# Up projection of a conditioned, quantised gated MLP: plain float32 products in place of three float32r products of high and low parts

## The reference

```python
scale = cond @ norm_w.T + 1.0                       # [32, 256]
ms = jnp.mean(x * x, axis=-1, keepdims=True)
h = x * (scale[:, None, :] * jax.lax.rsqrt(ms + EPS))
u = h @ up_w.T                                      # up_w [2048, 256]
val, gate = jnp.split(u, 2, axis=-1)
h = val * gelu(gate)                                # exact gelu, [.., 1024]
y = act_quant(h) @ weight_quant(down_w).T           # int8 rows, ternary weights
return y + x
```

## Time and profile before

| | |
|---|---|
| median of 2 runs | 430.2 us (430.07 to 430.33) |
| traced execution | 430.28 us, span 428.5 us |
| TensorE matmuls (PE) | 422.5 us busy, 99% of the span, 2081 records |
| TensorE weight loads (PEld) | 334.2 us, 78% |
| VectorE (DVE) | 283.4 us, 66% |
| ScalarE (ACT) | 189.6 us, 44% |
| GpSimd (POOL) | 192.1 us, 45% |

### The profile page before, as it was taken

How to read it: one execution, slowest core, us unless ns; L and a number is a source line. 1 busy time by engine, 2 the same in 40 slices (tenths; PEclk the granted TensorE clock), 3 DMA queues, 4 the chain that set the end, 5 groups by cost and what they waited for, 6 DMA issues and landing times.

```text
span 428.5 us, 7739 instructions
## 1 busy us (share of the span) xinstructions
PE 422.5 (99%) x2081; PEld 334.2 (78%) x2081; DVE 283.4 (66%) x539; ACT 189.6 (44%) x334; POOL 192.1 (45%) x323
## 2 busy tenths in 40 slices
PE   7999999999999999999999999999999999999997
PEld 5777777877877877777777777778778778777886
DVE  4887566576576575575675675665765765755776
ACT  5743444444444444444434444434444444444441
POOL 1565345345354354354454453453453543543520
PEclk9999999999999999999999999999999999999999
DMA  8424434334434334334244343244343344342324
GB/s 288 137 76 122 125 73 122 80 92 122 106 90 122 72 99 122 90 106 110 72 112 122 75 120 84 88 122 116 80 122 76 96 122 96 100 118 70 82 50 124
DMA packets 82024, 45.01 MB, mean 105 GB/s; under 512 B 68256, under 2 KB 68704, under 8 KB 81888
## 3 DMA queue, kind: packets, MB, share of 16 engines
q1 hardware_dynamic: 81584, 44.33, 40.0%
q10 hardware_dynamic: 432, 0.59, 0.4%
HBM read 20.00 MB, written 8.39 MB: 66 GB/s over the span
## 4 chain that ended last, share of the span: by engine, by line
PE 96%; DVE 1%; POOL 1%; DMA 1%; issue 0%; ACT 0%; DVEq 0%; POOLq 0%
PE p_gate L674 41%; PE p_val L674 41%; PE p_y L696 12%; PE p_gate L646 1%; PE p_val L646 1%; DMA cond_norm_sb<-cond_norm 1%; DVE y_sb L495 0%; PE p_gate L653 0%; POOL a_hi L306 0%; PE p_val L653 0%; POOL scaled L303 0%; PE p_y L621 0%; PE p_y L615 0%; DVE q_rounded L519 0%; DVE h L540 0%
## 5 line engine op out<-in xcount | busy, mean ns | idle before, releaser
L540 DVE SCALAR_TENSOR_TENSOR h<-p_val,rstd,gelu 128x512 f32<-128x512 f32 x128 | 95.4, 746 | 127.0 <-PE p_val L674 126.1
L384 ACT ACTIVATE gelu<-p_gate,rstd 128x512 f32<-128x512 f32 x128 | 88.1, 688 | 154.4 <-PE p_gate L674 144.0
L299 POOL TENSOR_TENSOR mean_sq_eps<-mean_sq,rms_eps 128x1 f32<-128x1 f32 x64 | 12.3, 192 | 213.1 <-PE p_val L674 198.8
L356 ACT ACTIVATE q<-q_rounded 128x1024 bf16<-128x1024 f32 x63 | 66.7, 1058 | 70.8 <-DVE q_rounded L578 70.8
L674 PE MATMUL p_gate<-up_hi,a_lo 128*128 128x512 f32 x248 | 83.0, 415 | 0.6 <-POOL a_lo L310 0.6
L564 DVE TENSOR_REDUCE h_max<-h 128x1 f32<-128x1024 f32 x63 | 76.9, 1220 | 2.2
L674 PE MATMUL p_val<-up_hi,a_hi 128*128 128x512 f32 x248 | 78.2, 396 | 0.0
L674 PE MATMUL p_gate<-up_hi,a_hi 128*128 128x512 f32 x248 | 78.1, 396 | 0.0
L674 PE MATMUL p_val<-up_hi,a_lo 128*128 128x512 f32 x248 | 78.1, 396 | 0.0
L674 PE MATMUL p_val<-up_lo,a_hi 128*128 128x512 f32 x248 | 78.1, 396 | 0.0
L674 PE MATMUL p_gate<-up_lo,a_hi 128*128 128x512 f32 x248 | 78.1, 395 | 0.0
(11 more groups left out here) (74 smaller groups left out, 249.3 us busy)
## 6 DMA issues: line engine op xcount, KB each, us to landing
xt_in<-x_t SPq DMA_DIRECT2D x32, 256.0 KB, 2.8
x_all<-x SPq DMA_DIRECT2D x32, 256.0 KB, 2.8
out<-y_sb SPq DMA_DIRECT2D x31, 256.0 KB, 2.2
up_raw<-up_w_t SPq DMA_DIRECT2D x6, 256.0 KB, 5.3
down_raw<-down_w_t SPq DMA_DIRECT2D x1, 1024.0 KB, 7.9
q_t<-q SPq DMA_TRANSPOSE x63, 3.1
up_raw<-up_w_t ACTq DMA_DIRECT2D x2, 256.0 KB, 3.3
out<-y_sb SPq DMA_DIRECT2D x1, 128.0 KB, 2.0
```

Source lines behind the costliest of these rows:

```text
L299: pool.tensor_tensor(mean_sq_eps[:, j:j + 1], mean_sq[:, j:j + 1], rms_eps[:, :], ALU.add).then_inc(pool_step, 1)
L356: act.activation(q[j % 2][:, :], q_rounded[j % 2][:, :], ACT.Copy, bias=-ROUND).then_inc(q_ready, 1)
L384: act.activation(gelu[c][:, :], p_gate[c][:, :], ACT.Gelu, scale=rstd[:, j:j + 1]).then_inc(gelu_done, 1)
L540: nc.vector.scalar_tensor_tensor(h[s][:, c * W:(c + 1) * W], p_val[c][:, :], rstd[:, j:j + 1], gelu[c][:, :], op0=ALU.mult, op1=ALU.mult). ...
```

## The change

The up products take the scaled x and the landed weights as they are, in plain float32: one product over two slices for a bank, 2 matmul calls in place of 6, 8 for a tile in place of 24. `a_hi`, `a_lo`, `up_hi`, `up_lo` and their semaphores are gone, and with them GpSimd's second multiplication and its subtraction, ScalarE's eight copies and VectorE's eight subtractions at the start, and `up_first`. Tiles 0 and 1 get their `scaled` from VectorE. The down products and everything behind the banks stay.

```diff
@@ GpSimd, tile
                 def product():
                     pool.tensor_tensor(scaled[s][:, :, :], xt_in[i][:, :, half, :], scale,
-                                       ALU.mult).then_inc(pool_step, 1)
-
-                    pool.tensor_tensor(a_hi[s][:, :, :], xt_in[i][:, :, half, :], scale,
-                                       ALU.mult).then_inc(pool_step, 1)
-
-                def low_part():
-                    pool.tensor_tensor(a_lo[s][:, :, :], scaled[s][:, :, :], a_hi[s][:, :, :].bitcast(fp32),
-                                       ALU.subtract).then_inc(a_ready, 1)
+                                       ALU.mult).then_inc(a_ready, 1)
...
@@ ScalarE, start
-            for c in range(NP * 2):
-                for k in range(KD):
-                    act.wait_ge(up_in[c * KD + k], 16)
-                    act.activation(up_hi[:, c, k, :], up_raw[:, c, k, :], ACT.Copy).then_inc(up_hi_ready, 1)
-                if c == 2:
-                    square(0, 0, True)
...
+            square(0, 0, True)
@@ VectorE, start
+            for j in range(2):
                 for k in range(KD):
...
+                    last = nc.vector.tensor_scalar(scaled[j][:, k, :], xt_in[0][:, k, j, :], scale_t[:, k, 0:1], None,
+                                                   ALU.mult)
                 last.then_inc(first_a_ready, 1)
...
-            for c in range(NP * 2 * KD):
...
-                nc.vector.tensor_tensor(up_lo[cols], up_raw[cols], up_hi[cols].bitcast(fp32),
-                                        ALU.subtract).then_inc(up_lo_ready, 1)
@@ TensorE, up
+                    if not (first and j == 0):
+
+                        pe.wait_ge(read, NP * (t - 1) + c + 1)
+                    for k in range(KD):
+                        if first and j == 0:
+
+                            pe.wait_ge(up_in[col * KD + k], 16)
+                        last = nc.tensor.matmul(bank[:, :], scaled[j % 2][:, k, :], up_raw[:, col, k, :],
+                                                start=(k == 0), stop=(k == KD - 1))
                     last.then_inc(done, 1)
```

More of the change, by code:

```diff
@@ L63, in build @@
         up_raw = sb("up_raw", [P, NP * 2, KD, W], fp32)
-        up_hi = sb("up_hi", [P, NP * 2, KD, W], fp32r)
-        up_lo = sb("up_lo", [P, NP * 2, KD, W], fp32r)
         down_raw = sb("down_raw", [P, KF, D], fp32)
@@ L82, in build @@
         scaled = [sb(f"scaled{i}", [P, KD, P], fp32) for i in range(2)]
-        a_hi = [sb(f"a_hi{i}", [P, KD, P], fp32r) for i in range(2)]
-        a_lo = [sb(f"a_lo{i}", [P, KD, P], fp32r) for i in range(2)]
         squares = [sb(f"squares{i}", [P, D], fp32) for i in range(2)]
@@ L137, in build @@
         scale_ready = sem("scale_ready")
-        up_hi_ready = sem("up_hi_ready")
-        up_lo_ready = sem("up_lo_ready")
         abs_ready = sem("abs_ready")
@@ L146, in build @@
         a_ready = sem("a_ready")
-        a_hi_ready = sem("a_hi_ready")
-        second_a_hi_ready = sem("second_a_hi_ready")
         squares_done = sem("squares_done")
@@ L279, in _ @@
             pool.wait_ge(scale_ready, 1)
-            BEFORE, PER_TILE = 3 + 2, 3
+            BEFORE, PER_TILE = 3 + 2, 1
             def tile(u, j, first):
@@ L319, in tile @@
                     product()
-                    pool.wait_ge(pool_step, step + 3)
-                    low_part()
+                    pool.wait_ge(pool_step, step + 1)
                 pool.tensor_tensor(rstd[:, j:j + 1], mean_sq_eps[:, j:j + 1], minus_half[:, :],
@@ L432, in _ @@
             dve.wait_ge(scale_ready, 1)
[L433 to L437, removed]
+            for j in range(2):
                 for k in range(KD):
-                    last = nc.vector.scalar_tensor_tensor(a_lo[j][:, k, :], xt_in[0][:, k, j, :], scale_t[:, k, 0:1],
-                                                          a_hi[j][:, k, :].bitcast(fp32),
-                                                          op0=ALU.mult, op1=ALU.subtract)
+                    last = nc.vector.tensor_scalar(scaled[j][:, k, :], xt_in[0][:, k, j, :], scale_t[:, k, 0:1], None,
+                                                   ALU.mult)
                 last.then_inc(first_a_ready, 1)
-            dve.wait_ge(a_hi_ready, KD)
-            low_part(0)
-            for c in range(NP * 2 * KD):
-                dve.wait_ge(up_hi_ready, c + 1)
-                cols = (slice(None), c // KD, c % KD, slice(None))
-                nc.vector.tensor_tensor(up_lo[cols], up_raw[cols], up_hi[cols].bitcast(fp32),
-                                        ALU.subtract).then_inc(up_lo_ready, 1)
-            dve.wait_ge(second_a_hi_ready, 1)
-            low_part(1)
             def ternary(stage):
@@ L624, in _ @@
             keep_busy(4)
[L626 to L655, removed]
             def up(u, j, c, first):
[L658 to L662, removed]
                 t = UNIT * u + j
-                if c == 0:
+                by_others = first and j < 2
+                if c == 0 and by_others:
+                    pe.wait_ge(first_a_ready, j + 1)
+                elif c == 0:
                     pe.wait_ge(a_ready, t - 1)
```

## The result

The changed kernel took 509.25 us, median of 2 runs (509.03 to 509.48), against 430.2 before: 1.184 times the time (95% interval 1.182 to 1.185). The forecast was 511 us, 1.19 times. The traced execution took 509.03 us, its span is 507.2 us.

A forecast was written before the change was run, and what follows sets the result against it. TensorE's stream was taken to bound the kernel, busy for 99% of the span. 430.28 us, plus 78.6 for tiles 2 to 63 and 2.0 at the start, gave 510.9: forecast 511 us, 1.19 times, range 506 to 552.

The forecast's parts named there:

- TensorE's stream is the time: Whole kernel: time is TensorE's stream plus a start and a tail; TensorE busy for 99% of the span.
- Sixteen records a tile: TensorE's up products: a plain float32 call becomes two matmul records, so 16 a tile against 24.
- Two streams per record: TensorE's up products: each record streams its 512 columns twice, 429 ns a record, 6.87 us a tile, 1.27 more.
- The float32r surcharge would not come back: TensorE's up products: plain float32 records pay 3 ns over their column slots, not float32r's 20 ns.
- Rival 1: TensorE's up products: surcharge stays, 467 ns a record (549 us, chance 0.24) or 447 ns (529 us, chance 0.17).
- The low level as a rival: TensorE in the loop: falls to its low level, 853 ns a record, 943 us; chance 0.04 with other dear cases.
- rival 3: TensorE stays at its low level, 853 ns a record, 943 us; chance 0.04 together with other dear cases.
- Start: Tiles 0 and 1: first up product at about 5.95 us, TensorE rises at 11.0, tile 2 begins at 22.4: +2.0 us.
- Down group: TensorE's down products in each tile: 8 bfloat16 matmuls, put as unchanged at 0.89 us.
- Rival 2: TensorE in the loop: one stream per record, 233 ns each, a tile of 4.63 us, 311 us; chance 0.07.
- VectorE with 4.24 us stays just beneath 4.63: Rival 2's loop: VectorE's 4.24 us of work a tile stays below TensorE's tile of 4.63 us.

The follow-up runs named there:

- e1: Kernel before with only the products of tiles 2 to 63 in plain float32, all splitting work kept: 507.8 us, ratio 1.181 to the kernel before.
- e4: Kernel before with its high and low parts in float16 instead of float32r, weights scaled by 1024: 402.6 us, ratio 0.936 to the kernel before.
- e6: Kernel before with every float32r product of tiles 2 to 63 in two matmuls of 256 columns: 435.0 us, ratio 1.011 to the kernel before.
- e2: The changed kernel run once more, nothing altered, to see when TensorE rises to its upper level: 508.8 us.
- e3: Kernel before without the product of a_lo and up_hi in tiles 2 to 63, 16 float32r matmuls a tile: 343.4 us, ratio 0.798.
- e7: e3 with ScalarE's rounding of the tile before (L356) moved behind the second gelu of a tile: 324.6 us, ratio 0.754 to the kernel before.

## Why the prediction was right

**TensorE's stream is the time: held.** e1 puts the loss of the loop on the products. The split work of the other engines was priced at zero and was worth 0.1 us in the loop.

**Sixteen records a tile: held**, read off two small plain float32 calls in the trace of before, and there are 1,024 at L598.

**Two streams per record: the price held.** It was argued from what the kernel's own split says of the multiplier, and no row of before showed it; the bounds from rows were 233 ns and 1.7 us (264 cycles over 32 columns are 8.25, not 8, so the upper one is 1.76; nothing rests on it). The spacing of 429 ns at 512 columns and 216 at 256 shows two slots a column. Whether a record passes its columns twice or takes each at half the rate would give the same spacing; no run tells the two apart. By the four passes that the Trainium skill states for true FP32 ("FP8 and Floating Point Precision", "TensorE Precision Notes") the trace agrees: a call costs 858 ns, four times 213.3 and two small fees.

**The float32r surcharge would not come back: held, and in part by luck.** The forecast chose 3 ns a record, not 20, because the surcharge was absent at the low level. That reason doesn't decide it: e4 shows that the small fee, which every kind of record pays at the upper level, is absent at the low level too, so a surcharge that is absent there may still be a fee. The row could not carry the weight of choosing between 429 and 447 ns. Rival 1 (467 or 447 ns) is excluded by 429. e4 and e6 show what the surcharge is tied to: 4-byte columns at one per slot, by column. What in the chip sets 0.45 ns a column is not shown.

**The low level as a rival: excluded.** Records at the low level, 853 ns apart, would have shown as rival 3; they lie 429 apart. The prediction called the granted clock of 1.00 in the earlier trace rows the sign that the upper level was held before. That column could not show it, as said under e2; the spacing of 233.5 ns does.

**Start: direction right, size off.** Forecast +2.0, measured +1.35. The first product came later than put (6.08 for 5.95, since VectorE's products of x waited for its transfer). TensorE rose at 9.5 us, where the forecast carried over 11.0 from the trace of before: 1.5 us less at half the rate take 0.75 us off, the later first product adds 0.13, and together they make up the difference. That the kernel before and the changed one rose at different times is chance as far as the runs show: the moment lay between 8 and 11 us with float32r starts alone.

**Down group: put at unchanged, 0.89; measured 7.742 - 6.869 = 0.87 us.** Tiles 2 to 63 hold 57 such groups, so this is 1.1 of the 1.2 us by which they came out cheaper than the 78.6 of the forecast. e4, without 4-byte records around the group, has 0.87 as well (6.05 less 24 x 0.216): the 0.02 us go with float32r neighbours. What they are wasn't examined.

**Rival 2 had the wrong price.** Had each record taken one slot a column, the time would have been about 343 us by e3, not 311. The step that failed is "VectorE with 4.24 us stays just beneath 4.63": it compared busy times, but what binds is a ring through VectorE and ScalarE of 5.0 us a tile, invisible while TensorE takes 6.49 (e7 opened it). Its sign and its chance didn't hang on that.

## What to carry to other kernels

Count operand parts before counting instructions: on this stream-bound TensorE three passes of split operands (5.60 us a tile) beat one plain float32 call (6.87), which costs four, even though each of the three pays a surcharge of its own. If the parts can be 2-byte numbers (5.18) the surcharge goes too. When an experiment or a change takes the bound away, look for the next one among the cycles of waits in the in-order programs; here busy shares put it 0.8 us a tile too low (4.24 against 5.0).

## What the runs showed that was not expected

- At the upper level a float32r record costs 0.45 ns a column (118 ns at 256 columns, 233.5 at 512), float16 0.42 (216 ns at 512); at the low level float32r shows no surcharge (425 ns at 512), and float16 no fee (425 too).
- TensorE reached its upper level between about 8 and 11 us in kernels whose TensorE work up to there was nearly the same; the rows of the loops, as far as shown, all lie at the upper level.
- With a product fewer, the order of two operations on ScalarE, which is idle for nearly half of the time, is worth 19 us of 343.
